# Window and linear attention with butterfly feed-forwards on one core: key halves merged inside PSUM, head outputs turned in place, matrices on ScalarE's queue

## What is computed

```python
x = x + attn_a(layernorm(x))   # window attention: 16 heads of 8, 2 key/value heads
x = x + ffn(layernorm(x))      # feed-forward 128 -> 512 -> 128 with butterflies
x = x + attn_b(layernorm(x))   # linear attention with elu(.)+1 features
x = x + ffn(layernorm(x))      # the same feed-forward weights

# attn_a, per block of 32 queries t and 64 padded keys u:
scores = einsum('bhntd,bhnud->bhntu', qb, kb)
win_mask = (u >= t) & (u < t + 32)
probs = softmax(where(win_mask, scores, -inf), axis=-1)
out = einsum('bhntu,bhnud->bhntd', probs, vb)     # then @ Wo + bo

# ffn: W_exp, butterfly (9 stages), gelu, butterfly (9 stages), W_con
```

## Time and profile before

| | us |
|---|---|
| median of 3 runs | 604.83 |
| lowest and highest run | 601.66, 607.39 |
| the profiled execution, its time | 608.12 |
| its span on the core, first to last instruction | 606.3 |
| PE busy in the span | 555.4 |
| DVE busy | 485.9 |
| POOL busy | 479.3 |
| ACT busy | 360.6 |

### The profile page before, as it was taken

How to read it: one execution, slowest core, us unless ns; L and a number is a source line. 1 busy time by engine, 2 the same in 40 slices (tenths; PEclk the granted TensorE clock), 3 DMA queues, 4 the chain that set the end, 5 groups by cost and what they waited for, 6 DMA issues and landing times.

```text
span 606.3 us, 16521 instructions
## 1 busy us (share of the span) xinstructions
PE 555.4 (92%) x6068; PEld 355.8 (59%) x6068; DVE 485.9 (80%) x1270; ACT 360.6 (59%) x634; POOL 479.3 (79%) x645
## 2 busy tenths in 40 slices
PE   2777688989989999999999999999999999999976
PEld 1443344545646575666757566666575666677754
DVE  6269998999898989898888989898988898843430
ACT  1343355656757577676676775767577666646532
POOL 5176568999987989989999989898999787856630
PEclk9989889999999999999999999999999999999998
DMA  6611110110001010100102011111010100000010
GB/s 220 216 36 27 23 29 23 29 44 13 24 25 40 25 46 23 44 27 23 47 13 55 9 43 27 41 29 40 23 50 4 40 11 20 2 18 18 2 36 17
DMA packets 37904, 22.48 MB, mean 37 GB/s; under 512 B 8384, under 2 KB 35520, under 8 KB 37824
## 3 DMA queue, kind: packets, MB, share of 16 engines
q1 hardware_dynamic: 36640, 19.93, 12.0%
q10 hardware_dynamic: 1184, 1.50, 0.8%
HBM read 15.91 MB, written 5.51 MB: 35 GB/s over the span
## 4 chain that ended last, share of the span: by engine, by line
PE 71%; DVE 17%; issue 6%; POOL 2%; ACT 1%; DMA 1%; DVEq 0%; POOLq 0%; ACTq 0%; SPq 0%
PE ring L548 17%; PE ring L536 17%; PE ps_o L521 8%; PE ps_s L504 8%; PE ring L485 6%; PE ring L559 4%; PE ring L579 3%; DVE merged L1064 3%; PE ring L619 3%; PE ring L568 2%; DVE o_w L1084 2%; DVE o_raw L1078 2%; PE ring L596 2%; DVE merged L1050 1%; DVE rowmax L1058 1%
## 5 line engine op out<-in xcount | busy, mean ns | idle before, releaser
L434 POOL TENSOR_TENSOR probs_t<-probs_m,first 128x1024 f32<-128x1024 f32 x64 | 157.4, 2461 | 7.9 <-ACT probs_m L834 7.8
L504 PE MATMUL ps_s<-kx,q_t 64*32 64x512 f32 x1024 | 71.4, 614 | 8.3 <-DVE merged L1050 8.0
L808 ACT ACT_TABLE_LOAD x58 | 74.4, 1283 | 4.7 <-issue 3.6
L825 ACT ACTIVATE merged<-ps_s 128x512 f32<-128x512 f32 x64 | 38.2, 596 | 57.9 <-PE ps_s L504 51.5
L521 PE MATMUL ps_o<-probs_t,vx 32*32 32x256 f32 x2048 | 70.3, 382 | 2.0 <-DVE o_raw L1078 2.0
L536 PE MATMUL ring<-xT_G,w1b 128*128 128x512 f32 x128 | 67.8, 620 | 1.4 <-ACT xT_G L796 1.3
L548 PEld LDWEIGHTS ring<-w,hid_F 128*128 128x128 f32 x512 | 59.2, 194 | 13.1 <-issue 12.5
L1064 DVE TENSOR_TENSOR merged<-merged,rowmax 128x512 f32<-128x512 f32 x64 | 65.8, 1028 | 0.1
L536 PE MATMUL ring<-xT_F,w1b 128*128 128x512 f32 x128 | 60.0, 608 | 3.5 <-DVE x_G L1040 1.8
L548 PE MATMUL ring<-w,hid_F 128*128 128x128 f32 x512 | 62.2, 280 | 0.4 <-ACT hid_F L818 0.4
L818 ACT ACTIVATE hid_G<-ring,b 128x512 f32<-128x512 f32 x64 | 44.0, 687 | 29.1 <-PE ring L536 26.4
(11 more groups left out here) (115 smaller groups left out, 1119.5 us busy)
## 6 DMA issues: line engine op xcount, KB each, us to landing
kx<-kv_rows SPq DMA_DIRECT2D x124, 40.0 KB, 2.2
x_P<-in_x SPq DMA_DIRECT2D x16, 256.0 KB, 3.0
out_x<-x_G SPq DMA_DIRECT2D x16, 256.0 KB, 2.5
vx_t<-kv_rows SPq DMA_DIRECT2D x128, 8.0 KB
down_s<-in_down_m SPq DMA_DIRECT2D x6, 256.0 KB, 5.6
up_s<-in_up_m SPq DMA_DIRECT2D x5, 256.0 KB, 5.6
kv_rows<-kv_t SPq DMA_DIRECT2D x16, 80.0 KB, 1.6
later<-in_later_c SPq DMA_DIRECT2D x1, 648.0 KB, 6.9
```

The costliest lines, as they stand in the source:

```text
L434: nc.gpsimd.tensor_tensor(probs_t[:, j % 2].rearrange("p u k h t -> p u (k h) t"), probs_m[:, j % 2].rearrange("p (a k) h t -> p a (k h) t ...
L504: last = nc.tensor.matmul(ps_s[32 * i:32 * i + 32, a], q_t[half, P * j + 32 * c:P * j + 32 * c + 32], kx[half, :, TSPAN * j + 32 * c:TSPAN ...
L808: nc.scalar.activation(unused[:, i:i + 1], half[0:1, 0:1], function)
```

## The change

- `first_half_out` is gone. The masked copy of `merge_halves` writes the second half over the first inside `ps_s`; row maximum and subtraction read `ps_s`, and the subtraction writes `merged` in SBUF and frees the bank.
- `head_outputs` transposes `ps_o` onto itself; reciprocal and product read it, and the product frees the bank. `o_raw` is gone.
- `load_butterflies` issues all fourteen matrices on ACT's queue; SP issues all eight key loads of group 0. `bo` moves from `later` to `first`, and the sum of the two feed-forward biases (`ffn_bias`) becomes a piece of its own on POOL in turn 2.
- All orders within a turn are new: where a turn begins, the banks of the ring, and the turns in which the butterfly products run (u stages in turns 0 and 1 instead of 0 to 3, d stages in 1 and 2 instead of 1 to 3; DVE's outer up stages in turn 2 instead of 3 and 4). There are 23 turns instead of 24.

```diff
@@ orders, shortened
 PRODUCTS = [
-    ("W.S2", 2, "S"), ("X.u6b", 3, "3", 0, 0), ("F.down", 4, "2"), ("X.u2b", 2, "1", 0, 0), ("G.xT", 6, "3"),
...
+    ("W.S3", 2, "S"), ("G.up3", 6, "0"), ("L.out1", 5, "1"), ("G.up0", 6, "3"), ("G.up2", 6, "2"),
+    ("W.oT", 3, "0"), ("L.oT", 5, "3"), ("X.u2b", 1, "2", 0, 0), ("G.up1", 6, "1"), ("X.d2", 2, "3", 0, 0),
+    ("X.u2a", 1, "2", 0, 0), ("P.q", 1, "2"), ("W.proj", 3, "0"), ("X.u3a", 1, "0", 0, 0), ("X.d3", 2, "1", 0, 0),
+    ("L.xT", 4, "3"), ("P.xT", 0, "1"), ("X.d0", 1, "2", 0, 0), ("X.u0a", 0, "0", 0, 0), ("L.proj", 5, "2"),
+    ("X.u3b", 1, "3", 0, 0), ("L.q", 4, "3"), ("W.PV0", 2, "T"), ("W.S0", 1, "S"), ("L.k0", 4, "0"),
+    ("L.k1", 4, "1"), ("X.d4", 2, "2", 0, 0), ("X.u4b", 1, "2", 0, 0), ("G.down", 6, "2"), ("F.xT", 3, "3"),
+    ("W.PV1", 2, "T"), ("X.u4a", 1, "1", 0, 0), ("X.u5b", 1, "1", 0, 0), ("W.S1", 1, "S"), ("F.up3", 3, "2"),
+    ("F.up0", 3, "1"), ("X.u6b", 1, "2", 0, 0), ("F.up2", 3, "3"), ("F.up1", 3, "2"), ("X.d5", 2, "1", 0, 0),
+    ("P.kv", 0, "1"), ("X.u0b", 0, "2", 0, 0), ("X.d1", 1, "2", 0, 0), ("L.kv", 4, "0"), ("W.PV2", 2, "T"),
+    ("X.u1b", 0, "1", 0, 0), ("W.S2", 1, "S"), ("G.xT", 5, "3"), ("X.u5a", 1, "0", 0, 0), ("L.out0", 4, "2"),
+    ("X.wT", 2, "3", 0, 0), ("X.u6a", 1, "1", 0, 0), ("F.down", 3, "0"), ("X.d6", 2, "0", 0, 0), ("X.u1a", 0, "1", 0, 0),
+    ("W.PV3", 2, "T"),
 ]
-TURNS = NG + 8
+TURNS = NG + 7
@@ SP's and ACT's loads
                 if g == 0:
                     sp.dma_start(first[:], first_c).then_inc(first_in, 16)
                     sp.dma_start(x_of(1, "P")[:], x_v[1]).then_inc(x_in[1], 16)
-                    load_butterflies(1, 3)
...
-                for h in range(HPK // 2 if g == 0 else HPK):
+                for h in range(HPK):
                     sp.dma_start(kx[h:P:HPK, h].rearrange("d (j n) -> d j n", j=TILES), keys_of(g)
                                  ).then_inc(kx_in.sem, 16)
...
-                for n in range(2):
+                for n in range(INNER):
+                    m = INNER - 1 - n
                     act.dma_start(up_s[n][:], up_m[n]).then_inc(up_in[n], 16)
-                act.dma_start(down_s[INNER - 1][:], down_m[INNER - 1]).then_inc(down_in[INNER - 1], 16)
+                    act.dma_start(down_s[m][:], down_m[m]).then_inc(down_in[m], 16)
@@ DVE, window attention
             def merge_halves(g, j):
...
-                dve.wait_ge(halved.sem, halved.after(g, f"W.c{j}"))
+                dve.wait_ge(product.sem, product.after(g, f"W.S{j}"))
+                merged_s, later_s = halves()
                 nc.vector.copy_predicated(
...
+                    merged_s, last_half.bitcast(mybir.dt.uint32).rearrange("p (a t) -> p a t", a=1)
+                    .to_broadcast([P, HEADS, WIN]), later_s).then_inc(vec.sem, 1)
             def row_max(g, j):
...
+                nc.vector.tensor_reduce(rowmax[:, j], halves()[0], AX_X, ALU.max).then_inc(vec.sem, 1)
+            def subtract_max(g, j):
...
+                nc.vector.tensor_tensor(merged[:, j % 2].rearrange("p k h t -> p (k h) t"), halves()[0], m, ALU.subtract
+                                        ).then_inc(drained["S"].sem, 1)
...
             def head_outputs(g, j):
...
-                nc.vector.transpose(o_raw[:, j % 2].rearrange("p k h r -> p k (h r)"), ps_o[:, :, 0:HPK * WIN]
-                                    ).then_inc(own.sem, 1)
+                nc.vector.transpose(ps_o[:, :, 0:HPK * WIN], ps_o[:, :, 0:HPK * WIN]).then_inc(vec.sem, 1)
+                o_raw = ps_o[:, :, 0:HPK * WIN].rearrange("p k (h r) -> p k h r", h=HPK)
...
-                    ALU.mult).then_inc(vec.sem, 1)
+                    ALU.mult).then_inc(drained["T"].sem, 1)
```

## The result

| | before | after |
|---|---|---|
| median, us | 603.82 (601.66 to 607.39, 4 runs) | 596.68 (595.42 to 597.42, 4 runs) |
| ratio of the runs | | 0.9866, 95% interval 0.9824 to 0.9907 |
| profiled execution: its span, us | 606.3 | 595.6 |
| DVE / POOL / ACT busy, us | 485.9 / 479.3 / 360.6 | 445.7 / 446.7 / 336.7 |

The change saves 1.3%, 7.1 us between the medians, where 19.6 us were forecast: 596.7 us instead of 585. Between the two profiled executions it is 10.7 us; that of before lay 3 to 4 us above its median.

A forecast was written before the change was run, and what follows sets the result against it. DVE, with tails on two-SBUF-input operations, was taken to pace the fill and PE the saturated turns; six turns (-0.8 + 6.9 + 5.6 + 2.5 + 2.7 + 2.7 = 19.6 us) off 604.8 gave 585 us, range 577 to 601.

The forecast's parts named there:

- Both tails: DVE's subtraction and head-output product lose the long durations of two SBUF inputs, taking 0.68 and 0.31 us.
- saturated turn: Later turns, PE busy throughout, stay at 32.5 us; DVE falls from 28.8 to about 26.3 us, hidden under PE.
- score bank: Held until the subtraction ends; tightest from S1 to S2, where it fits with 0.8 us to spare.
- key reload: Loading the next group's keys, 7.0 us from the end of S3 to S0, ends the first and second turn.
- First turn: S0(0) to S0(1), now with the u stages and DVE's outer stages (4.0 us): 19.1 us, 0.8 worse.
- Second and third turn: Fill turns without tails: 22.1 us (gain 6.9) and 24.0 us (gain 5.6).
- rival A: Start costs part of the fill's gain through loads, late ScalarE or PE's low clock: 8 us, 593 us; chance 0.17.
- Fourth and fifth turn: Fill turns set by PE's work plus some idle: 25.4 us (gain 2.5) and 28.9 us (gain 2.7).
- Drain: From S0(15) on, 117.8 us, the last group's chain keeps its order; nothing booked.
- start: Up to S0(0): ScalarE's first copy 0.7 us late, PE's u stages earlier; S0(0) at 24.8 us as before, nothing booked.
- Rival B: Fill: tails were not the pace; product, POOL and reload waits leave only 3 us gain, 602 us; chance 0.09.
- Rival C: Score bank becomes the bound if writing PSUM costs 1.0 us more per operation: PE stalls, 621 us; chance 0.08.

The follow-up runs named there:

- experiment 5: Changed kernel with both outer up stages' temporary in idle PSUM bank ps_o, the second directly after the first: 592.33 us, ratio 0.9761 to the kernel before.
- experiment 6: experiment 5 with the key loads of groups 1 to 4 issued from two queues, four from SP and four from ACT: 595.30 us, ratio 0.9803.
- experiment 13: experiment 11 with the load of the third group's input directly behind the first key spread, ahead of the constants: 589.99 us, ratio 0.9762.
- experiment 1: Changed kernel with only the first outer up stage's temporary in PSUM (ps_o) instead of u_tmp: 594.33 us, ratio 0.9797.
- experiment 10: experiment 5 with filler products on PE while it waits for keys, 16 ahead of S0(1) and 32 ahead of S0(2): 593.38 us, ratio 0.9835.
- experiment 15: experiment 5 with 16 filler products on PE ahead of S0(2) alone: 592.16 us, ratio 0.9785.
- experiment 7: experiment 5 with the matrices' loads issued from SP as in the kernel before: 594.41 us, ratio 0.9789.
- experiment 11: experiment 5 with all up matrices first on ACT's queue and four down matrices from SP behind the first key spread: 592.46 us, ratio 0.9817.
- experiment 9: Changed kernel with head outputs transposed into an SBUF buffer again, read there by reciprocal and product: 610.75 us, ratio 1.0126.
- experiment 14: Changed kernel with the load order of experiment 13 but outer stages left unmended: 595.52 us, ratio 0.9852.
- experiment 16: The changed kernel itself, unaltered, run again beside experiments 13 to 15: 597.77 us, ratio 0.9891.
- experiment 12: experiment 11 plus filler products on PE while it waits for keys: 591.48 us, ratio 0.9803.
- experiment 2: Kernel before, old order, with only the head outputs turned in place in PSUM: 601.21 us, ratio 0.9891.
- experiment 8: experiment 5 with the edits of experiment 6 and experiment 7 together: 599.84 us, ratio 0.9912.

## Why the prediction missed

**What held.** Both tails went (largest 0.69 and 0.29 us). Masked copy and in-place transpose cost 0.68 and 0.71 us on average for 0.72 and 0.70 taken. The saturated turn stayed 32.5 us with PE fully busy, and the score bank cost PE 4.3 us in the whole kernel. The direction held: 1.3% is over the 1% named. The key reload took 6.8 us from the end of S3(1) to S0(2) for 7.0 counted, and it ends the second turn (in experiment 5, as experiment 6 shows). The forecast's own first and second turn, 19.1 and 22.1 us, are what experiments 5 and 13 took (19.7 and 22.5; 19.9 and 22.2).

**First turn, the step that failed (+3.8 us).** The prediction moved the outer stages into the first turn, priced them at 4.0 us, as read in the second turn of before, and let the key reload end the turn, 12.1 + 7.0 = 19.1 us, with all of DVE's work behind S3 hidden under the 7.0. The 12.1 held: S3(0) ended at 37.14 us, 12.3 after S0(0). From there to S0(1) it took 10.6 us instead of 7.0, as S0(1) waited for the fourth subtraction behind the outer stages, and not for the keys. The prediction had just argued that an operation with two SBUF inputs has a tail beside POOL, and did not ask what POOL does at the new place. There POOL splits the first two blocks. The stages took 0.88 + 6.18 + 0.85 + 1.14 = 9.1 us; mended, the turn is 3.2 us shorter. By the Trainium skill, SBUF — State Buffer, section SBUF: two separate sides, the lock is taken by a VectorE operation with two SBUF inputs or in a two-port mode, and whichever engine starts first holds it for the whole instruction. The trace agrees for the first kind, 2.45 us at most here. The scalings of experiment 1, one input and SBUF to SBUF, were held too, 3.28 us for four; that they run in a two-port mode no row says.

**Second and third turn (+1.8, +2.1).** The forecast took PE's durations at the full clock. After the first turn's wait PE worked at the low level (clock 0.88 and 0.93 in the two turns); S0(1) to S1(1) took 5.8 us, in experiment 5 4.4 and in experiment 10, all at the high level, 3.5. In the third turn PE is in the chain, and 24.0 us had been right at full clock: 24.2 and 24.3 in experiments 10 and 15, 26.9 at 0.87 in experiment 5. At 0.93 it took 25.1 in experiments 7 and 11 and 26.1 in the changed kernel, whose PE was busy 22.9 us, 1.5 more than in experiment 10, and idle 3.2: the clock gives 1.5 of the 2.1 us, and the rest was not taken apart. A turn that does not wait for DVE any more is exposed to the clock, which the earlier trace rows had shown at 0.94 there. It was used for rival A only.

**Fourth and fifth turn (+2.4, +1.5).** PE's work was estimated at 24.6 and 28.5 us; it is 25.7 and 29.1, and PE idles 2.0 and 1.3 us where I had allowed 0.8 and 0.4. All versions of the new order but that of experiment 9 have 27.7 to 28.1 us in the fourth. No experiment took these terms apart.

**Drain (2.3 us not forecast) and start.** The last eight up products took 6.43 us before and 5.40 after, which accounts for 1.0; it is the clock, as the same eight take 5.40 or 3.70 in kernels that do not differ there. Changed kernel, then experiment 5:

```profile
582.00 5.40 PE L523 MATMUL ring<-xT_G,w1b 128*128 128x512 f32 x8 [0.75 <-ACT xT_G L780]
```

```profile
578.18 3.70 PE L523 MATMUL ring<-xT_G,w1b 128*128 128x512 f32 x8 [0.75 <-ACT xT_G L780]
```

These 1.7 us go into the totals: the drain takes 115.5 us in the profiled executions of the changed kernel and of experiments 1, 13, 14, 15 and 16, and 113.8 in those of 5, 7, 9, 11 and 12. So a difference of that size between the totals of two versions of the new order can be the drain's clock alone, and S0(6) has to be read beside it. The rest of the drain's gain over before, a little over 1 us, stays open: it is there with the head outputs alone in the old order (115.2 us in experiment 2) and in the new order without them (experiment 9).

The start came out at 24.83 us as booked, but not by the shifts counted. Timeline of the changed kernel, then a row of the kernel before:

```profile
11.15 0.57 ACT L774 ACTIVATE xT_P<-ring 128x512 f32<-128x512 f32 x1
...
13.23 0.34 SPq L319 DMA_DIRECT2D kv_rows<-kv_t  x1
17.47 5.08 SPq L328 DMA_DIRECT2D kx<-kv_rows  x8
...
24.83 1.09 PE L491 MATMUL ps_s<-kx,q_t 64*32 64x512 f32 x16
```

```profile
16.66 1.20 PE L639 MATMUL ring<-u_t,up_s 128*128 128x129 f32 x4 [4.52 <-issue]
```

ACT's first copy was 1.6 us later, not 0.7 (some loads took 0.55 to 0.75 us to issue), and the key rows landed 4.2 us after their issue beside the matrices, 1.6 before. On the other side PE's gap of 4.5 us ahead of 16.66, while ACT issued half of the first keys, is gone. Nothing booked for the start was right for this order of loads only: 1.0 to 3.1 us lay in it (experiments 14 and 13).

**Adding up.** The fill missed by 11.5 us. The drain's 2.3 us count the other way, and the profiled execution of before lay 3.3 us above the median it was set against, that of after 0.7. So the median missed by 11.5 too. The 596.7 us lie inside the stated range of 577 to 601, but by luck: no rival behind that range had the reason. Rival A (593) has the nearest price; its later start did not come, but PE at a low clock did cost, in the second and third turn. Rival B (602) said that the tails were not the pace; they were, and one of them came back at the moved stages. Rival C's mechanism was near: the prediction had 0.8 us to spare from S1 to S2, and in experiment 9 one tail of 2.1 us makes the score bank late for S3 in the saturated turn shown, and each such turn is 0.9 us longer.

## What to carry to other kernels

Taking the SBUF operand away from one operation does not remove all of its tail from the engine; a part can turn up at the next operation that GpSimd can hold: 5.7 of 30.7 us in experiment 2, 2.4 of 5.1 in experiment 1, 1.0 at the small sum in experiment 5. When an operation is moved, ask what the other engine on the shared side does at the new place, and price it with and without. Where a stage is paced by waits, price the products behind each wait at both clock levels; once the pacing engine is relieved, PE's work at the clock that it then has is a bound of its own.

## What the runs showed of the hardware

- A masked copy and a 32-block transpose of 128 x 512 floats within PSUM take 0.68 and 0.71 us, as from or to SBUF (0.68 to 0.72).
- Several operations in a row can be held for as long as GpSimd works: four of 0.28 us with both inputs in SBUF took 6.18 us, from 36.86 to 43.04, beside 4.75 and 1.14 us of GpSimd's work, which ended at 42.89. A scaling with one input, SBUF to SBUF, is held too: 3.28 us for four instead of 0.85.
- After the unfilled waits ahead of S0(1) the scores took 1.69 to 1.96 us in the changed kernel and experiments 1, 5, 9 and 13 to 16, and 1.09 in 6, 7, 8 and 11. In the third turn, behind the wait ahead of S0(2), the mean clock was 0.87 to 0.94 without fillers and 1.00 with them, every time, and the scores behind the fillers took 1.06 to 1.10. The same instructions of the start ran at either level in experiments 13 and 14.
- An 80 KB store issued 3.5 us behind the last of ScalarE's 17 loads took 4.2 us to land instead of 1.6.
- Of the 128 key loads of a kernel, 40 KB each, nearly all took 0.5 to 0.6 us to issue, and single ones up to 1.6 us in the changed kernel and 1.8 in experiment 5. In experiment 15 most turns have one above 1.1 us.
